# Copies of two heads' transposed probabilities on VectorE instead of ScalarE, in a cross-attention and local-attention kernel

## The reference

```python
q, k, v = split(shift_token(x) @ wqkv)        # 8 heads of 64
q, k = rotary_xpos(l2norm(q) * qs, l2norm(k) * ksc)
sim  = einsum('bhwid,bhwjd->bhwij', q * 8, look_around(k))   # windows of 128, own and previous
attn = softmax(where(mask, -max, sim))
o    = einsum('bhwij,bhwjd->bhwid', attn, look_around(v))
x    = x + o @ wo
x    = x + gated_gelu_mlp(layernorm(shift_token(x)))
```

## Time and profile before

| what | value |
|---|---|
| median of 3 runs | 772.15 us (772.13 to 774.22) |
| time of the profiled execution | 772.45 us |
| its span | 770.7 us |
| PE busy | 718.7 us, 93% |
| VectorE (DVE) busy | 498.9 us, 65% |
| ScalarE (ACT) busy | 494.3 us, 64% |
| GpSimd (POOL) busy | 462.6 us, 60% |

### The profile page before, as it was taken

How to read it: one execution, slowest core, us unless ns; L and a number is a source line. 1 busy time by engine, 2 the same in 40 slices (tenths; PEclk the granted TensorE clock), 3 DMA queues, 4 the chain that set the end, 5 groups by cost and what they waited for, 6 DMA issues and landing times.

```text
span 770.7 us, 16909 instructions
## 1 busy us (share of the span) xinstructions
PE 718.7 (93%) x4952; PEld 595.8 (77%) x4952; DVE 498.9 (65%) x1424; ACT 494.3 (64%) x1321; POOL 462.6 (60%) x646
## 2 busy tenths in 40 slices
PE   5989899899999999999999998999999999999957
PEld 4878787587878787878787867788787878787847
DVE  1376772785858585858585858666676767676732
ACT  3656634566666767676758686858585857575742
POOL 1467662695747474747575767757474747474722
PEclk9999995899999999999999999999999999999998
DMA  5664460150000000000000001010101010101000
GB/s 146 227 208 131 113 217 0 56 188 15 28 16 27 14 27 14 27 14 27 14 28 15 28 2 55 2 55 0 54 0 54 0 54 0 54 0 41 1 29 14
DMA packets 32795, 38.46 MB, mean 50 GB/s; under 512 B 8476, under 2 KB 22896, under 8 KB 32752
## 3 DMA queue, kind: packets, MB, share of 16 engines
q1 hardware_dynamic: 32752, 37.95, 15.5%
HBM read 29.55 MB, written 8.39 MB: 49 GB/s over the span
## 4 chain that ended last, share of the span: by engine, by line
PE 64%; issue 10%; DVE 9%; POOL 7%; ACT 7%; DMA 1%; ACTq 0%; DVEq 0%; POOLq 0%; SPq 0%
PE ps L448 35%; PE ps L655 5%; PE ps L614 4%; PE ps L641 3%; POOL pr L1494 3%; PE ps L632 2%; ACT pr L928 2%; PE ps L548 2%; PE ps L626 2%; PE ps L659 2%; PE ps L643 1%; PE ps L642 1%; PE ps L441 1%; DVE hT_lo L1189 1%; DVE arena L1052 1%
## 5 line engine op out<-in xcount | busy, mean ns | idle before, releaser
L1494 POOL TENSOR_SCALAR pr<-pr,rl 128x128 f32<-128x128 f32 (+1 forms) x256 | 108.7, 438 | 89.8 <-DVE rl L1222 89.5
L928 ACT ACTIVATE pr<-sm,mn 128x128 f32<-128x128 f32 (+1 forms) x256 | 113.5, 447 | 9.7 <-DVE mn L1216 9.0
L448 PE MATMUL ps<-hT_hi,w_hi 128*128 128x256 f32 (+1 forms) x352 | 105.3, 299 | 3.6 <-DVE hT_lo L1189 1.4
L1216 DVE CUSTOM_DVE_ANT_0 sm<-ps,wmask 128x128 f32<-128x128 f32 (+1 forms) x256 | 80.1, 354 | 33.8 <-PE ps L632 29.9
L448 PE MATMUL ps<-hT_hi,w_lo 128*128 128x256 f32 (+1 forms) x352 | 99.6, 283 | 0.0
L448 PE MATMUL ps<-hT_lo,w_hi 128*128 128x256 f32 (+1 forms) x352 | 99.2, 282 | 0.0
L888 ACT ACTIVATE sqb<-ps 128x512 f32<-128x512 f32 x64 | 38.0, 596 | 92.8 <-PE ps L448 90.3
L1464 POOL TENSOR_TENSOR rn<-ss,nhalf 128x16 f32<-128x16 f32 x32 | 95.2, 2975 | 2.7
L448 PE MATMUL ps<-wqkv_hi,yT_hi 128*128 128x512 f32 x192 | 78.8, 411 | 1.6 <-DVE arena L1073 1.6
L448 PE MATMUL ps<-wqkv_lo,yT_hi 128*128 128x512 f32 x192 | 75.9, 395 | 0.0
L448 PE MATMUL ps<-wqkv_hi,yT_lo 128*128 128x512 f32 x192 | 75.9, 395 | 0.0
(11 more groups left out here) (169 smaller groups left out, 2137.3 us busy)
## 6 DMA issues: line engine op xcount, KB each, us to landing
arena<-x SPq DMA_DIRECT2D x16, 256.0 KB, 3.0
ystream<-arena SPq DMA_DIRECT2D x16, 256.0 KB, 2.1
y_next<-ystream SPq DMA_DIRECT2D x16, 256.0 KB, 2.8
y_res<-ystream SPq DMA_DIRECT2D x16, 256.0 KB, 2.7
arena<-L_ffn_w SPq DMA_DIRECT2D x5, 640.0 KB, 4.7
arena<-ctx SPq DMA_DIRECT2D x8, 256.0 KB, 4.2
arena<-mask_BxSxS_ik SPq DMA_DIRECT2D x8, 256.0 KB, 3.4
xmid<-arena SPq DMA_DIRECT2D x8, 256.0 KB, 2.1
```

The costliest lines, as they stand in the source:

```text
L448: last = mm(out, lhsT(a), rhs(b), start=(start and i == 0), stop=(stop and i == 2))
L928: A(pr[:, h % NS, a:b], sm[:, h % NS, a:b], ACT.Exp, bias=mn[:, h, t:t + 1], scale=-1.0, accum_out=ls[:, h, t:t + 1]).then_inc(e_done, 1)
L1216: V.tensor_tensor_reduce(sm[:, h % NS, a:b], bank(h % SB)[:, a:b], wmask[:, a:b], 1.0, -NEG, ALU.add, ALU.min, mn[:, h, t:t + 1]).then_inc ...
L1494: G.tensor_scalar(pr[:, h % NS, a:b], pr[:, h % NS, a:b], rl[:, h, t:t + 1], 1.0, ALU.mult, ALU.mult).then_inc(pn_done, 1)
```

## The change

The copies `probs_T(h)` of heads 3 and 5 (the fourth and the sixth) go from ScalarE's program to VectorE's. They count a semaphore of their own, `pT_dve`. PE's waits for the copies are on both semaphores (`probs_copied`). In the hardware loops both waits always stand; in the steps written out the second one stands only where a copy of VectorE is meant.

```diff
+        pT_dve = sem("pT_dve")
+        DVE_HEADS = (3, 5)
+        ACT_HEADS = HEADS - len(DVE_HEADS)
...
+        def probs_copied(eng, s, h):
+
+            by_dve = len([i for i in DVE_HEADS if i <= h])
+            wait(eng, pT_done, ACT_HEADS * s + h + 1 - by_dve)
+            wait(eng, pT_dve, len(DVE_HEADS) * s + by_dve if by_dve or not isinstance(s, int) else 0)
...
-                        wait(pe, pT_done, HEADS * s)
+                        wait(pe, pT_done, ACT_HEADS * s)
+                        wait(pe, pT_dve, len(DVE_HEADS) * s)
...
-                        pe.wait_ge(pT_done, HEADS * s + h - 1)
+                        probs_copied(pe, s, h - 2)
...
-                    pe.wait_ge(pT_done, HEADS * s + 2 * pair + 2)
+                    probs_copied(pe, s, 2 * pair + 1)
...
-                        probs_T(h)
+                        if h not in DVE_HEADS:
+                            probs_T(h)
...
+                def probs_T(h):
+
+                    dve.wait_ge(pt_tr, HEADS * s + h + 1)
+                    wait(dve, pv_mm, HEADS * s + (h - 3 if h >= 4 else 0))
+                    V.tensor_copy(pT[:, h % 4, :], bank(3 + h % 2)[:, 0:3 * P]).then_inc(pT_dve, 1)
...
                         if h + 3 < HEADS:
                             row_min(h + 3)
+                        if h == 4:
+                            probs_T(3)
+                        if h == 6:
+                            probs_T(5)
```

## The result

The changed kernel takes 778.89 us in the median of 6 runs (778.44 to 780.58), the kernel before 772.20 on the same chip (6 runs). The ratio is 1.0088, with a 95% interval from 1.0074 to 1.0101. It is slower, as forecast, but by 6.7 us where 2.8 was forecast, and 778.89 lies above the range of 772.2 to 778.3.

What follows compares the result with a forecast made beforehand. PE bounds the kernel (64% of the span is its own work), with loss possible only in the attention part. Loop steps +1.8, waits +0.55, steps 1, 7 and 15 +0.25, step 0 +0.5, step 8 -0.26: +2.8, 775.0 us, range 772.2 to 778.3.

Steps and rivals of the forecast that it cites:

- Part 5: Second register waits on PE in loop steps: 0 to 0.16 us a step, taken as 0.05; elsewhere hidden behind matmuls.
- Part 4: PE's waits absorb 0.81 of 0.97 us, leaving 0.16 a step; head 5's copy just covered ahead of weighted(2), 379.97 against 379.98.
- The sum of the loop steps: 11 loop steps at 0.16 us, +1.8, and their added waits, 11 at 0.05, +0.55.
- Steps 1 and 7: Steps written out, priced with step 15: PE's waits up to 0.05 or 0.1 us longer, +0.25 for the three together.
- Step 0: Head 3's copy late in DVE's fuller queue, head 5's transposes 1.15 us later, partly absorbed: +0.5 us (bounds 0 and 1.15).
- Step 8: PE's 1.21 us wait for POOL's low part of wo, which starts after normalise(7), 0.27 us earlier: -0.26 us.
- rival 4: PE's idle time of about 0.9 us in every step lowers its clock: 0.96 us a step, 789 us; chance 0.03.
- Rival 2: Faster: ACT's 0.27 us reach PE at head 6's transposes in every step, -4.0, 768 us; chance 0.05.

Runs made afterwards that it cites:

- e1: Kernel before with all copies left on ACT, but heads 3 and 5 counting the second semaphore, so PE has the changed kernel's waits; ratio 1.0024 to the kernel before.
- e3: Changed kernel with PE waiting only for the semaphore of the engine that made the last copy at each place; ratio 1.0031 to the kernel before.
- e4: Changed kernel with only head 3's copy on DVE, head 5's back on ACT; ratio 1.0055 to the kernel before.
- e6: Changed kernel with head 3's copy ahead of row_min(7) and as many waits on PE as before the change; ratio 1.0000 to the kernel before.
- e2: Changed kernel with DVE's copy of head 3 ahead of row_min(7) instead of behind it; ratio 1.0035 to the kernel before.
- e8: The changed kernel, unedited, run and profiled a second time; ratio 1.0073 to the kernel before.
- e11: e7 with PE's waits for copies moved ahead of the late wait; ratio 1.0000 to the kernel before.
- e9: e1 with the line of PE's second wait repeated; ratio 1.0040 to the kernel before.
- e10: e1 with PE's waits for the copies ahead of the wait for POOL, and last in weighted; ratio 1.0006 to the kernel before.
- e7: Changed kernel, one wait per place, DVE's order: head 3's copy, row_min(7), row_sum(6), low_oT(0), head 5's copy, row_sum(7), low_oT(1); ratio 0.9974 to the kernel before.

## Why the prediction was right or wrong

- **Direction, and the wait on PE's path: right.** The idle time of ACT until DVE's minimum (0.39 us), DVE's copy of 0.55 us behind `row_min(7)`, the 0.92 us wait ahead of `weighted(1)`, and the end of the wait for POOL all appeared. Head 6's transposes were forecast 0.16 us late and came 0.15 us late in step 1 and in the first loop, and 0.24 late in the second, where the kernel before is 0.10 us earlier at them than in its first loop. Step 1 measured 0.17 us against a forecast of about 0.08.
- **Part 5, the waits: this term was mis-sized.** I took 0.05 us a loop step and 0.16 as the upper bound. They cost 0.18 by themselves (e1), and taking them out of the changed kernel gives back 0.22 and 0.25 (e3): 11 x 0.18 = 2.0 us instead of 0.55. The row that I read, a register wait that costs 0.08 us behind a late copy, was right, but I took it as the bound for a wait of any kind. The added wait also needs its value worked out, and both stand behind the late wait. And I named the wrong places. At head 2's transposes and `weighted(0)` nothing was lost: head 4's transposes start 5.20 us behind head 0's in either loop, where it was 5.28 and 5.18. What failed is that the waits elsewhere would hide behind matmuls in flight: at `weighted(2)` they did not.
- **Part 4, "just covered": failed in the loops, at the release.** The copy of head 5 ended 1.14 us after the start of its transposes, as computed (1.13), but `weighted(2)` started 0.24 us behind its end in the loop steps and 0.10 in step 1, where I had 0.07: 0.61 us behind head 6's transposes and not 0.47. With this copy on ACT (e4) it was 0.45. So the copy of head 5 held `weighted(2)`, one of the signs of being wrong that the prediction names. In the first loop the forecast lateness at head 6's transposes was right, and the missing 0.11 us a step arise here.
- **The sum of the loop steps** was +3.3 us measured and +2.3 forecast. Steps 1 and 7: +0.33 against 0.17. Step 0: +0.66 against 0.5, in a period that differs by 1.35 us between two profiles of the same kernel, so this agreement is luck.
- **Step 8: wrong sign.** PE did reach the product with `wo` earlier (its wait there fell from 1.21 to 0.73 us, as forecast), but the time was given back at PE's next wait, for ACT's normalised rows, which grew from 1.58 to 2.05 us; and behind it the clock was at half for 3.4 us. In place of -0.26 stands +1.16: some 0.17 at ACT's wait and some 1.0 behind it, about what the spell costs by e6 and e2. This is the largest single miss, 1.4 us. I had priced a gain at a wait without looking at the next wait behind it.
- **The clock (rival 4)** was named at the wrong place: the 0.9 us of idle time in every step never cost clock in the loops. The 2 us ahead of step 9's layer norm products went with a spell of 3.4 us.
- **The rest of 1.40 us ahead of step 0 and the 0.92 at the end** are not the change's as far as the runs show: spells of 3.4 us in the first 60 us come in some profiles (changed, e2, e3, e8, e11) and not in others, and step 15 with the rest takes 44.4 to 44.6 us in e1, e9 and e10 too, where no copy moved (changed 44.51, before 43.60).
- **Rival 2** was rejected for the right reason, the place in DVE's queue, but its price was wrong too: with the copy ahead of `row_min(7)` (e2) nothing was gained, because `row_sum(6)` also has to leave `low_oT(0)` behind it (e7), and then the gain is 0.18 to 0.34 us a step.

## What to carry to other kernels

When work moves to an idle engine, ask not how busy that engine is but what stands in front of the moved piece and what behind it: here each of two half-microsecond copies cost PE a wait, and the same copies in another order, with one wait per place, made the kernel 0.26% faster than it had been. Count a new semaphore as work on the waiting engine, and look in the trace which record carries the late wait: in a hardware loop, register arithmetic and a separate wait behind a late release cost 0.18 us a step, and one wait per place on the last producer is enough where the engine's own order covers the rest. A gain ahead of a wait is worth only what the next wait lets through.

## What the runs showed of the hardware that was not expected

- A wait's price depends on what stands behind it. With an ALU_OP and an EVENT_SEMAPHORE behind a late release, PE's weight load came 0.22 us after POOL's end instead of 0.05 (e1). A repeated wait that fell on the same EVENT_SEMAPHORE added nothing there (e9); an additional EVENT_SEMAPHORE behind a late copy moved the product from 0.10 to 0.25 us behind the copy's end.
- The order of waits works in opposite directions: the late one last gained 0.25 us a step in the first loop against e1 (39.10 to 38.85), and cost 0.13 us in step 1, whose values are constants (38.96 to 39.09). At head 6's transposes the cheaper order is in both cases the one in which PE's weight load itself carries the late wait.
- In this kernel 3.4 us at half clock followed idle times of 1.98 to 2.12 us in four profiles of four, and none followed the 0.9 us that recur in every step of the changed kernel.
